# DLRM tower in FP32 on one core: two Gram pieces with two samples a matmul, a new order of the queues behind the look-ups, and three tiles' second bias on DVE

## The reference

```python
e = jnp.stack([tbl_f[ids[:, f]] for f in range(26)], axis=1)     # 512 x 26 x 128
sd = jnp.einsum('bfd,bd->bf', e, dense)                          # 26
ss = jnp.einsum('bfd,bgd->bfg', e, e); pairs = ss[:, iu, ju]     # 325, upper triangle
h = jnp.concatenate([dense, sd, pairs, dense], axis=1)           # 607
h = jnp.maximum(h @ W_top1 + b_top1, 0.0)                        # 512
h = jnp.maximum(h @ W_top2 + b_top2, 0.0)                        # 256
y = h @ W_top3                                                   # 1
```

## Time and profile before

| | |
|---|---|
| three runs | 102.73, 103.72, 107.73 us; median 103.72 |
| the profiled execution | 104.4 us, its span 102.6 us |
| mean granted TensorE clock | 0.966 |
| busy share of the span | PE 89%, DVE 73%, ACT 60%, POOL 63% |
| instructions | PE 1440 matmul records and as many weight loads |

### The profile page before, as it was taken

How to read it: one execution, slowest core, us unless ns; L and a number is a source line. 1 busy time by engine, 2 the same in 40 slices (tenths; PEclk the granted TensorE clock), 3 DMA queues, 4 the chain that set the end, 5 groups by cost and what they waited for, 6 DMA issues and landing times.

```text
span 102.6 us, 3385 instructions
## 1 busy us (share of the span) xinstructions
PE 90.9 (89%) x1440; PEld 76.1 (74%) x1440; DVE 74.7 (73%) x179; ACT 61.7 (60%) x131; POOL 65.0 (63%) x70
## 2 busy tenths in 40 slices
PE   4998689999999999999928579899999998997991
PEld 4966268878888888888727379788988886896870
DVE  0269699999999999997008879793868749859211
ACT  1633449469559649429608697793868749747110
POOL 2678777777777777787777777777777776000000
PEclk9999999999999999999996559999999999999999
DMA  1899996944934999321222222122222222000000
GB/s 27 225 241 407 379 374 139 401 149 99 397 122 77 361 400 343 103 51 46 54 61 61 53 58 56 53 58 51 58 51 58 51 58 58 26 3 6 0 0 1
DMA packets 6465, 13.37 MB, mean 130 GB/s; under 512 B 1969, under 2 KB 3122, under 8 KB 6450
## 3 DMA queue, kind: packets, MB, share of 16 engines
q1 hardware_dynamic: 4112, 8.95, 24.7%
q0 software_dynamic: 2048, 4.20, 15.9%
q10 hardware_dynamic: 290, 0.01, 0.2%
HBM read 13.15 MB, written 0.00 MB: 128 GB/s over the span
## 4 chain that ended last, share of the span: by engine, by line
PE 70%; ACT 8%; DMA 8%; issue 6%; DVE 3%; SPq 2%; DVEq 0%
PE hidden L357 18%; PE gram L386 15%; PE gram L357 14%; DMA raw<-in_tables_one 8%; PE hidden L413 7%; PE stage L341 7%; ACT Z L512 5%; PE second L430 5%; DVE Z L589 2%; PE hidden L402 2%; ACT ET L490 2%; PE stage L413 1%; PE second L428 1%; ACT part L479 1%; SPq L273 1%
## 5 line engine op out<-in xcount | busy, mean ns | idle before, releaser
L310 POOL DMA_INDIRECT rows<-in_tables_gather,idx x64 | 64.3, 1004 | 20.9 <-issue 18.9
L589 DVE COPY Z<-gram 32x112 f32<-32x112 f32 (+3 forms) x72 | 23.1, 320 | 11.8 <-PE gram L386 10.9
L572 DVE TENSOR_SCALAR onehot<-ids,rowid 128x1024 fp32r<-128x1024 int16 (+1 forms) x48 | 29.6, 668 | 1.7 <-DMA ids<-in_ids_one 1.7
L512 ACT COPY Z<-gram 32x112 f32<-32x112 f32 (+1 forms) x72 | 23.2, 322 | 11.7 <-PE gram L386 10.3
L357 PE MATMUL hidden<-onehot,part 128*128 128x512 f32 x80 | 20.5, 401 | 1.2 <-DVE onehot L572 0.7
L357 PE MATMUL gram<-onehot,part 128*128 128x512 f32 x80 | 20.4, 403 | 0.6 <-DVE onehot L572 0.6
L386 PE MATMUL gram<-ET 128*32 128x27 f32 x1024 | 14.9, 202 | 5.5 <-issue 4.4
L386 PEld LDWEIGHTS gram<-ET 128*32 128x32 f32 x1024 | 12.5, 117 | 8.5 <-issue 6.2
L357 PEld LDWEIGHTS hidden<-onehot,part 128*128 128x128 f32 x80 | 14.4, 188 | 5.2 <-DVE onehot L572 1.5
L357 PEld LDWEIGHTS gram<-onehot,part 128*128 128x128 f32 x80 | 15.0, 193 | 4.1 <-DVE onehot L572 1.0
L579 DVE TENSOR_TENSOR part<-raw,part 128x512 fp32r<-128x512 f32 (+2 forms) x20 | 13.3, 678 | 1.8 <-ACT part L479 1.0
(11 more groups left out here) (40 smaller groups left out, 49.0 us busy)
## 6 DMA issues: line engine op xcount, KB each, us to landing
raw<-in_tables_one SPq DMA_DIRECT2D x9, 512.0 KB, 4.9
ids<-in_ids_one SPq DMA_DIRECT2D x4, 256.0 KB, 6.9
rows<-in_tables_gather,idx POOLq DMA_INDIRECT x64, 3.6
W1s<-in_W_pairs SPq DMA_DIRECT2D x1, 768.0 KB, 7.5
W1d<-in_W_dense SPq DMA_DIRECT2D x1, 512.0 KB, 5.1
W2s<-in_W_top SPq DMA_DIRECT2D x1, 512.0 KB
raw<-in_tables_one SPq DMA_DIRECT2D x1, 384.0 KB, 3.7
ids<-in_ids_one SPq DMA_DIRECT2D x2, 128.0 KB, 4.1
```

The source lines that it names most:

```text
L310: pool.indirect_dma_start(out=rows[:, m % ROWS_RING, :], out_offset=None, in_=x["tables_gather"], in_offset=bass.IndirectOffsetOnAxis(ap=i ...
L512: last = act.copy(dst, src)
L572: dve.tensor_scalar(onehot[:, m % RING, 0:w], ids16[:, B * SIDE[g][0]:B * SIDE[g][0] + w], rowid[:, k:k + 1], None, ALU.is_equal).then_inc ...
L589: last = dve.tensor_copy(dst, src)
```

## The change

- Pieces 0 and 1 take two samples a matmul: 64 columns of weights, 54 moving columns (both samples' 27 vectors), 64 partitions of output, of which the two diagonal blocks are used. A piece then needs 16 groups of 64 columns, two banks: piece 0 has both `gram` banks, piece 1 both `hidden` banks. Piece 3 may start when piece 0 is moved, as piece 2 may.
- The order of PE, ACT and DVE behind the look-ups is written out, with another sequence. ACT empties stage banks ahead of or behind whole moves, no longer in their middle.
- For tiles 0 to 2 the bias of layer 2 is no longer put in by PE; DVE adds it ahead of the last layer, from `b2b`, which one more transfer of 128 KB fills. Tile 3 keeps the two matmuls.

```diff
+DOUBLE = 0, 1
+DGROUP = 64
...
-        gram = [pb(f"gram{i}", [P, 512]) for i in range(2)]
-        hidden = [pb(f"hidden{i}", [P, 512]) for i in range(2)]
+        gram = pb("gram", [P, 1024])
+        hidden = pb("hidden", [P, 1024])
...
+        def gram_of(p):
+            if p in DOUBLE:
+                return (gram, hidden)[p][:, 0:PIECES[p][1] // 4 * DGROUP]
+            return gram[:, 512 * (p % 2):512 * (p % 2) + PIECES[p][1] // 4 * NV]
... (z_moves)
-                    src = gram[p % 2][32 * i:32 * i + 32, 0:size // 4 * NV].rearrange(
-                        "p (j c) -> p j c", c=NV)[:, :, q:q + 4 * (ns - 1) + 1:4]
+                    first = q + (i % 2 * NV if p in DOUBLE else 0)
+                    src = gram_of(p)[32 * i:32 * i + 32, :].rearrange(
+                        "p (j c) -> p j c", c=DGROUP if p in DOUBLE else NV)[:, :, first:first + 4 * (ns - 1) + 1:4]
... (sync)
+            sp.dma_start(b2b[:, :], x["b_top2"].rearrange("(o n) -> o n", o=1).broadcast_to([P, H2])).then_inc(w2_in, 16)
... (gram_ready)
-                if PIECES[p][0] == P:
+                if p == 1:
                     pe.wait_ge(look_taken, NO + 1)
                 if p >= 2:
-                    pe.wait_ge(gram_act, p - 1)
-                    pe.wait_ge(gram_dve, p - 1)
+                    pe.wait_ge(gram_act, 1 if p == 3 else p - 1)
+                    pe.wait_ge(gram_dve, 1 if p == 3 else p - 1)
... (gram_piece)
+                    if p in DOUBLE:
+                        for i in range(2):
+                            b = b0 + 4 * j + 2 * i
+                            last = pe.matmul(gram_of(p)[64 * i:64 * i + 64, DGROUP * j:DGROUP * j + 2 * NV],
+                                             ET[:, VP * b:VP * (b + 2)], ETv[:, b:b + 2, 0:NV], start=True, stop=True)
... (layer1_dense, tile 0, chunk 0)
-                    pe.wait_ge(look_taken, NO + 1)
+                    pe.wait_ge(gram_act, DOUBLE[-1] + 1)
+                    pe.wait_ge(gram_dve, DOUBLE[-1] + 1)
... (layer2)
-                    for n in range(2):
-                        pe.matmul(at, ones[:, :], b2h[:, n, :], start=(n == 0), stop=False)
+                    if t == T - 1:
+                        for n in range(2):
+                            pe.matmul(at, ones[:, :], b2h[:, n, :], start=(n == 0), stop=False)
... (last_layer)
+                h2 = second[t % 2][:, 0:H2]
+                if t < T - 1:
+                    dve.tensor_tensor(h2b[:, :], h2, b2b[:, :], ALU.add).then_inc(h2_biased, 1)
+                    dve.wait_ge(h2_biased, t + 1)
+                    h2 = h2b[:, :]
```

More of the change, by code:

```diff
@@ L156, in dlrm_tower @@
         h2w = sb("h2w", [P, H2])
+        h2b = sb("h2b", [P, H2])
         y = sb("y", [P, T])
@@ L212, in dlrm_tower @@
                 (3, 6): ["b4"], (4, 3): ["b5"], (4, 7): ["b6"], (5, 7): ["b7"]}
-        SOON = {1: ["b8"], 2: ["b9"], 3: ["b10"], 4: ["b11"], 5: ["b12"]}
-        AMONG = {5: ["b13"], 6: ["b14"], 7: ["b15"]}
-        STAGED = [s for g, k in sorted(AMID) for s in AMID[g, k]] + [s for n in range(NP) for s in SOON.get(n, []) + AMONG.get(n, [])]
+        THEN = [f"b{n}" for n in range(8, NB)]
+        STAGED = [s for g, k in sorted(AMID) for s in AMID[g, k]] + THEN
         def bank_of(name):
@@ L251, in layer1_bank @@
         def layer1_bank(t, c):
-            return ([*hidden, *stage][c] if t == T - 1 else hidden[c % 2])[:, 0:P]
+            if t == T - 1 and c >= 2:
+                return stage[c - 2][:, 0:P]
+            return hidden[:, 512 * (c % 2):512 * (c % 2) + P]
         def taken(t, c):
@@ L383, in gram_piece @@
                 for j in range(size // 4):
[L384 to L387 removed]
+                    if p in DOUBLE:
[3 more added lines that the diff above has]
+                                             ET[:, VP * b:VP * (b + 2)], ETv[:, b:b + 2, 0:NV], start=True, stop=True)
+                    else:
+                        for i in range(4):
+                            b = b0 + 4 * j + i
+                            last = pe.matmul(gram_of(p)[32 * i:32 * i + 32, NV * j:NV * (j + 1)],
+                                             ET[:, VP * b:VP * (b + 1)], ETv[:, b, 0:NV], start=True, stop=True)
                 last.then_inc(gram_done, 1)
@@ L552, in _ @@
             act.wait_ge(w1d_in, 32)
-            for p in range(NP):
-                move_gram(p)
-                for name in AMONG.get(p, ()):
-                    empty_stage(name)
-                if layer1_of(p):
-                    take_odd(*layer1_of(p)[1])
+            move_gram(0)
+            move_gram(1)
+            move_gram(2)
+            empty_stage("b8")
+            take_odd(0, 1)
+            empty_stage("b9")
+            move_gram(3)
+            take_odd(0, 3)
+            empty_stage("b10")
+            move_gram(4)
+            take_odd(1, 1)
+            empty_stage("b11")
+            take_odd(1, 3)
+            empty_stage("b12")
+            move_gram(5)
+            take_odd(2, 1)
+            empty_stage("b13")
+            move_gram(6)
+            empty_stage("b14")
+            take_odd(2, 3)
+            move_gram(7)
+            empty_stage("b15")
+            move_gram(8)
             for c in (1, 3):
```

107 lines of the change are left out of this document (71 added, 36 removed).

## The result

The changed kernel takes 113.53 us, the median of 4 runs (113.14 to 113.99), beside 104.39 us for the kernel before. The ratio is 1.100, with a 95% interval of 1.088 to 1.112: 10% slower. The prediction was 109.6 us (103.5 to 113.0). The direction was right, the size was not: 9.1 us were lost where 5.9 were forecast.

The account below looks back on a forecast made before the run. PE's queue behind the look-ups, starved for code, bounds the kernel. Last transposes 88.4 plus waits 6.0 is 94.4; plus tail 12.9, span 107.3; clock +1.2, 108.5; execution +1.8, 110.3; median 0.7 lower, 109.6 us (103.5 to 113).

Parts of the forecast that it names:

- waits 1 to 3: PE idle behind pieces 4, 5 and 6, waiting for copies, folds or an emptied bank: 1.5, 3.0 and 1.5 us.
- The blocks of code: PE's code behind the look-ups arrives in blocks of 256 instructions, none passed faster than in 3.7 to 4.0 us.
- POOL slipped: POOL's gather 44 waits for batch 8's later transposes: 0.8 us, up to 2 at half clock, hidden.
- The tail: From the last batch's transposes on PE to the span's end: 12.9 us, against 12.6 before.
- DVE's adds: Three bias adds of 128x256 on DVE for tiles 0 to 2: 0.45 us taken, 0 on the path.
- the doubled piece: Pieces 0 and 1 on PE: 1.5 us each, between 0.9 and 3.0; hidden by the fetch up to 1.85 each.
- The rival by which two wide matmuls do not overlap: Pieces 0 and 1 take 3.0 us each and the next block is asked for late: 111.4 us, chance 0.12.
- g2 waits for m0 … hidden too: Piece 2 waits for piece 0's copies until 54.9 us, early enough for the code resumption at 57.65: no cost.
- no pause for code behind g3: After the four bare pieces, code pauses add nothing, since layer work takes longer per instruction and doesn't starve.
- the clock term, +1.2: PE's clock stays low or falls later until about 61.75 us, slowing work behind: +1.2 us, bounds 0 and +3.0.
- the second fall: Rival: the clock falls again in the 3.0 us wait of tile 2's first chunk: +2 to +3.5, 112.4 us, chance 0.15.
- the bias: PE loses two layer-2 matmuls for each of tiles 0 to 2, before the last batch's transposes: 1.3 us less.

Follow-up runs that it names:

- all_but_order: Changed kernel with the old sequences of PE, ACT, DVE and POOL put back, doubled pieces and DVE's bias kept: 103.08 us, ratio 0.984 to the kernel before.
- order_alone: Kernel before with only the new sequences of PE, ACT and DVE, single pieces and PE's bias for every tile: 117.37 us, ratio 1.121.
- the shift test: Changed kernel with ten warming matmuls made three, 28 instructions fewer, where the kernel before takes about 132 us: 134.74 us, repeated 134.05 us, ratio 1.015.
- double_alone: Kernel before with pieces 0 and 1 doubled, nothing else: 102.89 us, ratio 0.982.
- double_shifted: Kernel before with pieces 0 and 1 doubled and 28 instructions fewer at its start: 102.73 us, ratio 0.992.
- changed_control: The changed kernel itself, unedited, run again beside its variants: 113.16 us, ratio 1.083 to the kernel before.
- changed_moves_first_3: Changed kernel with ACT moving pieces 4 and 5 ahead of emptying the stage bank: 111.68 us, ratio 1.068 to the kernel before.
- changed_filler_3: Changed kernel with three matmuls nobody reads in PE's wait inside tile 2's first hidden chunk: 111.63 us, ratio 1.064 to the kernel before.
- changed_b8_early: Changed kernel with batch 8's transposes between pieces 1 and 2, to free POOL: 112.77 us, no ratio.
- changed_moves_shifted: Changed kernel with ACT moving pieces 4 and 5 first and 28 instructions fewer at its start: 107.57 us, ratio 1.039 to the kernel before.

## Why the prediction was right or wrong

**Right: the direction, and the mechanism.** The order is the loss (all_but_order 0.984, order_alone 1.121), by waits 1 to 3 and by starving for code. The three waits measured 1.49, 2.85 and 1.27 us for 1.5, 3.0 and 1.5. The blocks of code are as read from the earlier trace rows: x125 and x128 in order_alone, the shift test moved their ends, and q8's transfers stand 2.4 to 2.9 us ahead of the resumptions. The Trainium skill (Runtime: NRT & Kernel Launch, Instruction fetch mechanics) calls the crossing of a block mostly hidden; here the pauses are 2.03 and 1.83 us, so the trace disagrees in this stretch. POOL slipped, by 2.5 us (gather 44 at 64.44 instead of 61.93) rather than 0.8 to 2, and it was hidden as said. The tail was 13.2 for 12.9. DVE's adds take 0.42 us each, for 0.45.

**Too low, and partly saved by luck: the doubled piece.** 1.88 us instead of 1.5. The text said that up to 1.85 the fetch hides it; g1 is cut by the block's end anyway, and its pause is only 0.45 us. But g2's start hangs on the end of g0, through m0: it came out right (55.01 against 54.9) because g0 began at 49.91, 0.3 us ahead of the 50.2 in the sum, which made up for the 0.4 that g0 took longer. The rival by which two wide matmuls do not overlap (3.0 us) is out. The Trainium skill (TensorEngine Tiling (Array Packing), When to Use Tiling) gives 2x column tiling at 64 columns and 4x at 32. Taken on the prediction's 3.0 us for columns one behind another, 2x gives an estimate of 1.5 us and not the 3.0 to 3.5 that the prediction drew from it. The trace's 1.88 us for a 64-column piece is a factor of 1.6, its 1.77 us for a 32-column piece only 1.7: it agrees roughly at 64 and disagrees at 32.

**Wrong, the first failed step: "g2 waits for m0 … hidden too".** Start and length of the wait were right (55.01 against 54.9); that it costs nothing was not. The sum took each resumption as so long after the last one. In the trace, 58.98 − 55.01 = 3.97 us lie between g2's start and the next resumption: the time runs from where PE gets past its own wait, not from the entry at 54.20 (4.78). Likewise 62.81 − 58.98 = 3.83, and in double_alone 58.55 − 55.15 = 3.40. The first two lie near the 3.73 and 4.03 of the earlier trace rows, the third is shorter. I read it as the next block being asked for only behind the wait. The transfers bear this out: the one that ends the pause at 58.98 stands at 56.1, 1.9 us behind the entry but 1.1 us behind g2's start, just as those of the kernel before stand 1.1 to 1.4 us behind its resumptions. In the seven further profiles of kernels with this g2 (double_alone, double_shifted, changed_control, changed_moves_first_3, changed_filler_3, changed_b8_early, changed_moves_shifted) a transfer stands 1.0 to 1.4 us behind g2's start. The exception is all_but_order: its transfer stands at 53.8, ahead of g2's start at 55.13, and no pause cuts its g2. So the request can also come ahead of the wait; what decides that is open, and no run took g2's wait away on its own. Its price: g3 over at 63.05 instead of 61.75, 1.3 us.

**Wrong, the second: no pause for code behind g3.** The prediction counted the blocks only through the four bare pieces and took it that layer work doesn't starve. g6 follows 1.0 us of layer-2 work and had its block end in it: 2.76 us (90.82 to 93.58) instead of 1.8, 1.0 us more. In the control's profile g6 runs whole (x128), so this one comes and goes from one execution to the next; with the moves first it is 1.95, with the shift it is gone. The transfer stands at 90.7 in the changed kernel's profile and at 87.6 in the control's, of the same code. A count by hand would thus have given the place, 120 records into g6, but not whether a pause stands there; why the request comes 3 us apart is open.

**Wrong, the third: the clock term, +1.2.** Its first part holds: the clock was low until 66.0, in which b8 took 1.12 where the earlier trace rows have 0.66, and from b8's start to g4's end (63.05 to 71.68, against 62.25 less 0.5 to 69.1 by the sum) this cost 8.63 − 7.35 = 1.3 us. But the second fall, a rival at 0.15 that was left out of the sum, came as well: 4.70 us from (2,0)'s start to g6's (86.12 to 90.82) where full speed gives 3.0 (0.67 + 0.89 + 0.5 + 0.95), 1.7 us. It was put at +2 to +3.5, of which the lower end, 3.4 us of work at half clock, had no row behind it; measured are 3.5 us (86.5 to 90.0). The filler shows that the gap causes it. This was an error in kind: the sum itself had a bare 3.0 us wait in it, and treated what that wait does to the clock as another case, not as a part of the same one.

The account up to b15: 94.4 + 1.3 (g2's wait in the block time) + 1.3 (first clock fall) + 1.7 (second) + 1.0 (g6) − 0.4 (waits a little shorter) = 99.3, against 98.99 measured. With the forecast's 1.2 for the clock, the error of 3.4 at b15 is the late block 1.3, the second fall 1.7 and g6 1.0, less 0.6 of small terms. The rest of 3.7 (113.99 against 110.3 for the profiled execution) is 0.3 in the tail.

**Not as told: the bias.** The sum took 1.3 us off for it. Alone it moved b15 by 0.1 us in its profile and the median not at all: the saved matmuls became waits for ACT and for code. Whether the 1.3 were real inside the new order was not tried by itself.

**Left open.** Some 4 us remain over all_but_order when the moves are first and the blocks shifted (107.57 against 103.08, beside 106.14 and 104.88 us for the kernel before). Its three waits (0.71, 1.92, 1.49) sum to 4.1, where the old order had 0.6 (the 0.6 of the earlier trace rows); no kernel took them away with the new order kept, so that these are the rest is an account and not a test.

## What to carry to other kernels

Between a piece and the first reader of its copies keep as much other work of PE as the copies, the fold and the take need together (here some 5 us), and price a wait that you let in twice: its own length and, at 2.85 us of idle PE, another 1.5 to 1.7 us for the low clock behind it. Where a queue is starved for code, count instructions: fewer and wider ones win (0.982 for 128 matmul records of 54 columns instead of 256 of 27), a block end's place can be worth some 2 us (0.983 in the slow surroundings, for 28 instructions less at the start), and bare stretches of short instructions should not stand next to one another.

## What the runs showed of the hardware that I had not expected

- The pause for code depends on waits as well as on the count: the transfer of the next block stands 1.1 us behind the end of PE's wait for m0 (56.1 against 55.01), and PE resumes 2.9 us behind it, at 58.98. all_but_order, with its transfer ahead of the wait, is the exception.
- The instruction queue's transfers can be read in the profile and tell such a pause from others.
- The same kernel before took 104 to 106 us at some times and 132 us at others, on chip 0 both, with PE getting on there in steps of about 0.7 us or a double of it, while no block arrives. Variants of the new order that cost 6 to 7% otherwise (the moves first, the filler) cost 1 to 2% there, and the 28 instructions saved gain 1.7% there on the kernel before.
- A matmul record of 128x54 in two column groups has 1.88/64 = 29 ns where a 128x27 one in four has 1.77/128 = 14 ns: twice the columns for twice the time. A piece takes 6% more time (1.88 against 1.77 us) with half the instructions.
- 2.7 us of useless matmuls in place of idle PE made the kernel 1.5 us faster.
